# Window attention: maximum and exponentials of the next unit ahead of the sums and casts of this one, and one load issued later

## What is computed

```python
def _L1_attn_ref(x, Wq_sem, Wk_sem, Wq_geo, Wk_geo, Wv, Wo, logit_scale):
    ...
    scores = scores * jnp.exp(logit_scale)[None, :, None, None]
    mask = k_pos[None, :] <= pos[:, None]
    scores = jnp.where(mask[None, None], scores, NEG_INF)
    probs = jax.nn.softmax(scores, axis=-1)
    out = jnp.einsum('bhqk,bhkd->bhqd', probs, v2)
    out = out.transpose(0, 2, 1, 3).reshape(Bq, Tq, H * DV)
    return out @ Wo
```

## Time and profile before

| | us |
|---|---|
| median of 3 runs | 2266.08 |
| lowest, highest | 2265.18, 2269.56 |
| the profiled execution, its own time | 2264.35 |
| its span in the trace | 2262.6 |
| `window_stage`: opening, from first load to first maximum | 1461.2 to 1514.0 |
| `window_stage`: loop, to the last `attend` | 1514.0 to 1579.3 |
| `window_stage`: last `attend` and output projection | 1579.3 to 1594.8 |

### The profile page before, as it was taken

The page is one execution under the profiler, slowest core; times in us unless marked ns, Lnnn a source line. Parts: engine busy times, 40 slices in busy tenths (PEclk is TensorE's granted clock), DMA queues, the critical chain, the costliest instruction groups (busy, mean ns, idle before and its releaser), DMA issues. The chain is left out here.

```text
span 2262.6 us, 34573 instructions
## 1 busy us (share of the span) xinstructions
PE 1862.6 (82%) x10272; PEld 1514.9 (67%) x10272; DVE 1249.9 (55%) x2155; ACT 794.6 (35%) x1666; POOL 893.5 (39%) x644
## 2 busy tenths in 40 slices
PE   3399999999999698894536883786699999997996
PEld 2189999999999333342215662676598899985775
DVE  5145555555555588987418311355365666564887
ACT  3122222222222245643203110234366666662121
POOL 0512121121211254445205275021577777773554
PEclk7589999999999898997768896787899999998998
DMA  6420101010111401222380013200478887885564
GB/s 221 173 77 29 57 28 56 28 56 28 46 38 48 155 20 55 70 79 80 118 310 28 1 48 109 110 1 1 172 276 278 278 281 280 284 283 199 180 207 149
DMA packets 97647, 279.17 MB, mean 123 GB/s; under 512 B 13506, under 2 KB 15136, under 8 KB 94240
## 3 DMA queue, kind: packets, MB, share of 16 engines
q1 hardware_dynamic: 80320, 228.29, 28.9%
q0 software_dynamic: 17248, 49.86, 6.7%
HBM read 210.39 MB, written 67.71 MB: 123 GB/s over the span
## 5 line engine op out<-in xcount | busy, mean ns | idle before, releaser
L619 DVE TENSOR_TENSOR rffn_h<-rffn_ps_hidden,rffn_silu 128x128 f32<-128x128 f32 x272 | 79.4, 292 | 301.4 <-ACT rffn_silu L592 301.4
L592 ACT ACTIVATE rffn_silu<-rffn_ps_hidden 128x128 f32<-128x128 f32 x272 | 75.6, 278 | 458.7 <-PE rffn_ps_hidden L667 458.7
L628 DVE TENSOR_TENSOR rffn_y<-rffn_ps_y,rffn_y 128x512 f32<-128x512 f32 x272 | 188.0, 691 | 3.0 <-PE rffn_ps_y L686 1.1
L667 PE MATMUL rffn_ps_hidden<-rffn_w0h,rffn_xsh 128*128 x544 | 156.7, 288 | 7.3 <-issue 4.6
L561 POOL TENSOR_TENSOR rffn_w1l<-rffn_raw,rffn_w1h 128x768 fp32r<-128x768 f32 x32 | 59.2, 1851 | 254.4 <-ACT rffn_w1h L581 254.4
L667 PE MATMUL rffn_ps_hidden<-rffn_w0h,rffn_xsl 128*128 x544 | 154.5, 284 | 0.0
L667 PE MATMUL rffn_ps_hidden<-rffn_w0l,rffn_xsh 128*128 x544 | 153.9, 283 | 0.0
L667 PE MATMUL rffn_ps_hidden<-rffn_w1h,rffn_xsl 128*128 x544 | 153.9, 283 | 0.0
L667 PE MATMUL rffn_ps_hidden<-rffn_w1h,rffn_xsh 128*128 x544 | 153.6, 282 | 0.0
L667 PE MATMUL rffn_ps_hidden<-rffn_w1l,rffn_xsh 128*128 x544 | 153.1, 281 | 0.0
L561 POOL TENSOR_TENSOR rffn_w0l<-rffn_raw,rffn_w0h 128x768 fp32r<-128x768 f32 x32 | 58.8, 1840 | 221.2 <-ACT rffn_w0h L581 221.2
(11 more groups left out here) (618 smaller groups left out, 5905.9 us busy)
## 6 DMA issues: line engine op xcount, KB each, us to landing
moe_raw<-in_moe_w SPq DMA_DIRECT2D x47, 769.5 KB
moe_raw<-in_moe_w SPq DMA_DIRECT2D x47, 768.0 KB, 5.4
rffn_raw<-in_ffn_w SPq DMA_DIRECT2D x16, 1536.0 KB, 6.8
ys<-moe_y SPq DMA_DIRECT2D x47, 512.0 KB
xs<-route_zero SPq DMA_DIRECT2D x17, 256.0 KB
rffn_x_in<-xs SPq DMA_DIRECT2D x17, 256.0 KB, 3.1
ys<-rffn_y SPq DMA_DIRECT2D x17, 256.0 KB, 2.0
y<-in_x SPq DMA_DIRECT2D x4, 1024.0 KB
```

The lines of the kernel that those rows point to most:

```text
L592: nc.scalar.activation(sil[n % 2][:], hb[n % 2][:, 0:P], ACT.Silu).then_inc(s_sil, 1)
L619: nc.vector.tensor_tensor(h32[n % 2][:], hb[n % 2][:, P:GU], sil[n % 2][:], ALU.mult).then_inc(s_h32, 1)
L628: nc.vector.tensor_tensor(y[:, t, :], yb[n % 2][:], y[:, t, :], ALU.add).then_inc(s_yadd, 1)
L667: last = nc.tensor.matmul(hb[n % 2][:], xs[p][:, c, t * P:(t + 1) * P], w[j][q][:, bass.ds(mine + c * GU, GU)], start=(c == 0 and m == 0), ...
```

## The change

Two edits, on three engines' lists. VectorE: `shift(0)` stands ahead of the loop, and iteration u does `shift(u + 1)`, `inverse(u)`, `probs_low(u - 1)` where it did `shift(u)`, `probs_low(u - 1)`, `inverse(u)`. ScalarE: `exps(0)` stands ahead, and iteration u does `probs_high(u - 1)`, `exps(u + 1)`, `probs(u)` where it did `exps(u)`, `probs_high(u - 1)`, `probs(u)`. SyncE: the load of `rawT` is issued last of the seven, after a wait for both `xw` loads. Every instruction is kept; no buffer and no other wait is changed.

```diff
@@ -2156,11 +2156,12 @@
-            sp.dma_start(rawT, A["att_qT"]).then_inc(s_rawT, 16)
             sp.dma_start(ident[:], A["ident"]).then_inc(s_const, 16)
             sp.dma_start(scale[:], A["att_scale"]).then_inc(s_const, 16)
             sp.dma_start(rope[:], A["att_qrope"][:, W0:NT, :, :]).then_inc(s_const, 16)
             sp.dma_start(wmask_raw, A["att_wmask"]).then_inc(s_const, 16)
+            sp.wait_ge(s_xw, 32)
+            sp.dma_start(rawT, A["att_qT"]).then_inc(s_rawT, 16)
@@ -2248,10 +2249,12 @@
+            exps(0)
             for u in range(2 * HKV):
-                exps(u)
                 if u:
                     probs_high(u - 1)
+                if u + 1 < 2 * HKV:
+                    exps(u + 1)
                 probs(u)
                 if u >= 3 and u % 2:
                     out_high((u - 3) // 2)
@@ -2377,11 +2380,13 @@
+            shift(0)
             for u in range(2 * HKV):
-                shift(u)
+                if u + 1 < 2 * HKV:
+                    shift(u + 1)
+                inverse(u)
                 if u:
                     probs_low(u - 1)
-                inverse(u)
                 if u >= 3 and u % 2:
                     out_low((u - 3) // 2)
             probs_low(2 * HKV - 1)
```

## The result

| | before | changed |
|---|---|---|
| median, us (runs on the same chip) | 2265.63 (10) | 2278.01 (10) |
| lowest, highest | 2262.22, 2274.7 | 2272.73, 2285.89 |
| profiled execution, its own time | 2264.35 | 2273.23 |
| its span | 2262.6 | 2271.4 |

The ratio is 1.0051, with a 95% interval of 1.0034 to 1.0068: 12.4 us more by the medians, 11.6 by the ratio. The forecast was 2275.3, between 2269.5 and 2281, slower at 0.80. The two profiled executions differ by 8.9 us.

The account below looks back on a forecast made before the run. The prediction took a chain VectorE, ScalarE, VectorE to bound the loop before, and one through TensorE's turn and scores after. Loop +7.2 and load +2.0 give +9.2 us: 2273.6 for the profiled execution, median 2275.3, range 2269.5 to 2281.

Parts of the forecast that it names:

- The ring: Loop: maximum, sums, low parts, TensorE's turn, its scores, next maximum, nothing overlapping; iterations 9.8 and 8.3 us, `turn(6)` +7.2 us.
- Turn and scores: TensorE in the loop: 4.5 us after 5.3 us idle (turns 1, 2, 4), 3.0 behind an `attend` (turns 3, 5).
- Behind `turn(6)`: Loop's end: `attend(2)`, `turn(7)` (7.36 us later) and `attend(3)` (another 2.95) keep their lengths.
- The load: Opening: `rawT` lands 2.6 us later, about 1471.7, and TensorE's products at L2432 start 2.0 us later.
- The later end: Opening: +3.3 us if `rawT` takes the identity's 6.4 us from issue to landing.
- The rule by which the products follow GpSimd's low parts: Opening: VectorE's last L2299 cannot pass before GpSimd finishes at 1486.9; L2306 ends 2.1 us later, products start 0.25 after.
- The sum: Whole kernel: +7.2 in the loop and +2.0 in the opening make +9.2 us, median 2275.3 us.
- Rival 1: Loop: low clock also behind an `attend`, each turn and scores 4.65 us; total +13.2, 2279.3 us; chance 0.18.
- Rival 2: Loop: full clock everywhere, turn and scores 3.0 us after idle; total -1.5 to +0.5, about 2265.6 us; chance 0.16.
- Rival 3: Loop: scores ready for every maximum, VectorE sets 5.2 us an iteration, `turn(6)` about 1557.6, total 2256.7 us; chance 0.04.

Follow-up runs that it names:

- e2_load_only: Kernel before with only the later `rawT` load, after the wait for both `xw` loads: 2269.37 us against 2263.47, ratio 1.0029.
- e8_load_last_no_wait: Kernel before with `rawT` issued last but without the wait for the `xw` loads: 2269.72 us against 2264.77, ratio 1.0021.
- e3_scores_ahead: Changed kernel with old load order and TensorE making scores(u + 2) ahead of turn(u): 2251.79 us against 2263.47 before, ratio 0.9949.
- e4_fill: Changed kernel with old load order and 24 unread matmuls in each TensorE gap ahead of turns 1, 2, 4, 6: 2265.99 us, ratio to before 1.0009.
- e6_low_first: Changed kernel with old load order and VectorE's probs_low(u - 1) ahead of inverse(u) again: 2276.61 us against 2264.77 before, ratio 1.0058.
- e7_out_later: Changed kernel, old load order, scores(u + 2) ahead of turn(u), out_high and out_low one iteration later: 2252.28 us against 2264.77 before, ratio 0.9945.
- e1_loop_only: Kernel before with only the new order of VectorE and ScalarE, loads in old order: 2272.22 us against 2263.47, ratio 1.0035.

## Why the prediction was right, point by point

- **The ring.** Right in every link. From a maximum to the next turn 5.26 us were worked out, and 1528.73 - 1523.47 is 5.26. The maximum waits for the scores, the wait for the casts is gone, and undoing TensorE's order alone turns the loss into a gain.
- **Turn and scores.** 4.5 us were taken behind idle time and 3.0 behind an `attend`. Measured, to VectorE's next maximum: 4.68, 4.88, 4.92 and 5.63 for turns 0, 1, 2 and 4 (here the 0.04 is in), and 3.10 twice. The term was sized from the two long forms in the trace of before, 4.3 and 4.65, and was too small by 0.1 to 1.1 us each time: the low clock held over more of the work. Together that is 2.0 us, and it is why `turn(6)` came 9.3 us late in place of 7.2.
- **Behind `turn(6)`** the lengths were kept as they were. They moved: to the last `attend` 9.3 us in place of 10.3, since the clock rose sooner, so that the loop's total is +8.3. The last `attend` itself took 5.2 us in place of 3.7, with the low clock in its middle. No edit accounts for that: `e2_load_only` and `e8_load_last_no_wait` show the same with the old loop, and `e3_scores_ahead`, `e4_fill` and `e6_low_first` took 3.7 with the new one. Its cause stays open.
- **The load.** The step that was too small is "some 4.9 to 5.35 us later, about 1471.7: 2.6 us later than now". The two token loads took 5.8 us to land in place of 5.35, and `rawT` then took 6.06 from its issue, so it was 3.9 us late. The later end that was given, by the identity's 6.4 us from issue to landing, was the right size: it puts `rawT` 3.85 us late and the products 3.3 (in part by luck: `xw` landed 0.4 us later and `rawT` 0.3 sooner behind it). The products moved by 3.6 in place of 2.0, just beyond that end. That `xw` gains nothing held too: the identity landed 4.4 us after its issue in place of 6.4, but `xw` no earlier. The rule by which the products follow GpSimd's low parts, and a VectorE instruction stretched beside them, held: the last L2302 took 2.71 us in place of 0.69. With the page "DMA: Bandwidth & Descriptors" of the Trainium skill, section "Anatomy of one DMA", the load would have cost 4.4 us; the traces, 6.06 us here and 6.98 in `e2_load_only` from issue to reading, speak against using that estimate for this issue path.
- **The sum.** +3.6 and +8.3 and +1.5 (the last `attend`) are 13.4 us; the medians say 12.4. The forecast's 9.2 lies below for the two sizes named, which erred the same way; the last `attend`'s 1.5 it did not have. That the two profiles differ by 8.9 only is chance in both directions: the execution profiled before lost 3 us to a low clock in the opening that no other did, and the stage began 2.2 us earlier in the changed one, while the rest behind the stage took 0.7 us longer (13.4 - 3.0 - 2.2 + 0.7 = 8.9).
- **Rival 1**, a low clock everywhere, did not come: both turns behind an `attend` ran at 1.00. **Rival 2**, a full clock everywhere, did not come either, and `e4_fill` shows that its price was near the truth: with every long turn but `turn(0)` made short, the total was 1.0009 of before (0.9996 to 1.0022). **Rival 3** was tried with its condition in `e3_scores_ahead`, and its 1557.6 for `turn(6)` (43.6 us after the first maximum) met the measured 43.9. But its terms do not add up to that: six iterations of 5.2 us behind the forecast's `turn(0)` at 1520.43 end at 1551.6. The other 6 us it does not name; measured, the two iterations with an `attend` took 3.3 us more than 5.1 each, as TensorE's own work stands in the way (`e7_out_later`).

## What to carry to other kernels

Where engines work in program order, running one engine ahead pays only if what it then waits for is also made ahead: ask of the first instruction of the new iteration who makes its input, and behind what that stands in the maker's list. Here the same edit costs 8 us with TensorE's old order and is worth 11.5 below the start with two of its lines swapped, while the swap alone gives 4.5. And a profile of before is one draw of the clock: one stretch of TensorE's was 12% longer in it than in any other profile. Here turn and scores took 4.7 to 5.6 us behind idle gaps of 4.6 to 5.3 us, where 4.5 were taken; the length with all of them at the low clock, 5.6, is the bound to reckon with.

## What the runs showed of the hardware

- Extra matmuls with no use made the kernel faster: 96 of them in four gaps kept the granted clock at 1.00 in the turns and scores that followed, which then took 3.1 us in place of 5.0 to 5.6 (in `e1_loop_only`), and the kernel's median fell from 2272.22 to 2265.99.
- The same 137 back-to-back matmuls took 26.8 us in one execution and 23.5 to 24.0 in all others, by how long the clock stood low in it. The instructions were equal, and the idle time just ahead of them, 3.9 us in the slow one, was 4.8 to 6.0 us in the others; so this cannot be read off the order.
- A load of 1 MB, issued once two loads of half the size had landed, was read 6.06 us after its issue in the changed kernel and 6.98 in `e2_load_only`, longer than the 5.8 and 5.7 us in which those two had landed from the first one's issue. Among other loads it had taken 6.96 us (before) and 6.86 (`e8_load_last_no_wait`).
